# Decoder layer with routed experts on one core: second half's scatter and first half's gather sent one DMA to an expert block, ranks made at tile 11, first block turned behind the last values

## The reference

```python
x = _layernorm(x + attn(x, Wq, Wk, Wv))
x = _layernorm(x + xattn(x, ctx, ctx, mask, Wq, bq, Wk, bk, Wv, bv, Wo, bo))
logits = x @ Wg + bg
topk_vals, topk_idx = jax.lax.top_k(logits, 2)
topk_w = softmax(topk_vals)
h = relu(einsum('bsd,edf->bsef', x, W1) + b1)      # 8 experts, f = 512
eo = einsum('bsef,efd->bsed', h, W2) + b2
y = sum(take(eo, topk_idx) * topk_w) + x
return gamma * (y - mean(y)) * rsqrt(var(y) + 1e-5) + beta
```

## Time and profile before

| what | value |
|---|---|
| median of 3 runs | 957.79 us (957.04 to 963.1) |
| the profiled execution | 955.7 us, span 953.9 us |
| PE busy | 765.7 us, 80% of the span |
| DVE busy | 628.2 us, 66% |
| ACT busy | 457.6 us, 48% |
| POOL busy | 303.2 us, 32% |
| chain that ended last, by engine | PE 59%, DVE 19%, issue 6%, POOL 6%, DMA 5%, ACT 2% |
| indirect DMAs, scatter | 32, mean 982 ns on POOL |
| indirect DMAs, gather | 32, mean 952 ns on POOL |

### The profile page before, as it was taken

How to read it: one execution, slowest core, us unless ns; L and a number is a source line. 1 busy time by engine, 2 the same in 40 slices (tenths; PEclk the granted TensorE clock), 3 DMA queues, 4 the chain that set the end, 5 groups by cost and what they waited for, 6 DMA issues and landing times.

```text
span 953.9 us, 14840 instructions
## 1 busy us (share of the span) xinstructions
PE 765.7 (80%) x4736; PEld 375.7 (39%) x4736; DVE 628.2 (66%) x983; ACT 457.6 (48%) x919; POOL 303.2 (32%) x311
## 2 busy tenths in 40 slices
PE   6767999889999999999888859853994997699700
PEld 3433222222222222222235536532682775477500
DVE  3568788778888888888548977874361432296346
ACT  2211677667777777777665243422341442245300
POOL 6000086967000000000135562737005003264074
PEclk9978899999999999999999979985996999799955
DMA  7661629796504040400007000002222223212231
GB/s 224 164 179 52 146 95 280 251 263 251 89 1 89 1 80 11 77 13 2 0 1 329 23 1 1 0 12 85 76 74 105 69 67 93 87 57 68 85 88 44
DMA packets 53682, 86.64 MB, mean 91 GB/s; under 512 B 16425, under 2 KB 41257, under 8 KB 52457
## 3 DMA queue, kind: packets, MB, share of 16 engines
q1 hardware_dynamic: 41689, 53.25, 20.3%
q0 software_dynamic: 9280, 31.20, 9.9%
q10 hardware_dynamic: 2640, 1.24, 0.6%
HBM read 48.15 MB, written 33.03 MB: 85 GB/s over the span
## 4 chain that ended last, share of the span: by engine, by line
PE 59%; DVE 19%; issue 6%; POOL 6%; DMA 5%; ACT 2%; SPq 2%; POOLq 0%; DVEq 0%; ACTq 0%
PE bank L475 10%; PE bank L483 10%; PE quad L784 10%; PE quad L458 9%; PE bank L798 7%; DVE rowmax L856 6%; PE bank L589 3%; POOL yg L1585 2%; PE quad L560 2%; POOL x_sorted L1535 2%; DVE max L962 2%; DVE sc L957 1%; DVE xres L931 1%; ACT probs L1279 1%; DMA qstack<-negrows 1%
## 5 line engine op out<-in xcount | busy, mean ns | idle before, releaser
L856 DVE TENSOR_REDUCE rowmax<-quad 128x1 f32<-128x1024 f32 x256 | 303.4, 1219 | 73.0 <-PE quad L458 71.6
L1279 ACT ACTIVATE probs<-bank 128x512 f32<-128x512 f32 x512 | 281.7, 595 | 101.3 <-PE bank L475 99.2
L475 PE MATMUL bank<-qstack,kstack 98*128 98x512 bf16 x512 | 194.1, 387 | 15.2 <-ACT probs L1279 9.7
L458 PE MATMUL quad<-kstack,qstack 96*128 96x512 bf16 x512 | 177.3, 386 | 9.2 <-DVE rowmax L856 7.8
L483 PE MATMUL bank<-probs,vslot 128*32 128x512 f32 x1024 | 138.1, 608 | 0.0
L784 PE MATMUL quad<-xbT,w_all 128*128 128x128 bf16 x1104 | 102.6, 226 | 33.4 <-issue 30.5
L475 PEld LDWEIGHTS bank<-qstack,kstack 98*128 98x128 bf16 x512 | 49.0, 97 | 199.4 <-ACT probs L1279 168.9
L784 PEld LDWEIGHTS quad<-xbT,w_all 128*128 x1104 | 76.5, 97 | 60.2 <-issue 45.6
L1388 ACT ACTIVATE xbT<-bank 128x512 bf16<-128x512 bf16 x46 | 27.5, 597 | 138.0 <-PE bank L765 98.5
L1521 POOL TENSOR_TENSOR lnv<-lnv,power 128x4 f32<-128x4 f32 (+1 forms) x8 | 9.6, 1198 | 264.3 <-DVE lnv L909 264.3
L458 PEld LDWEIGHTS quad<-kstack,qstack 96*128 96x128 bf16 x512 | 48.4, 99 | 70.8 <-DVE rowmax L856 34.2
(11 more groups left out here) (169 smaller groups left out, 976.3 us busy)
## 6 DMA issues: line engine op xcount, KB each, us to landing
w_all<-w_split SPq DMA_DIRECT2D x2, 4096.0 KB, 17.5
kstack<-k_parts SPq DMA_DIRECT2D x48, 128.0 KB, 7.2
xb<-x_sorted SPq DMA_DIRECT2D x46, 128.0 KB, 2.2
y_sorted<-ysb SPq DMA_DIRECT2D x46, 128.0 KB, 1.7
x_sorted<-zeros POOLq DMA_DIRECT2D x6, 768.0 KB, 9.0
vslot<-v_all SPq DMA_DIRECT2D x8, 512.0 KB, 8.8
w1raw<-in_w POOLq DMA_DIRECT2D x8, 512.0 KB, 5.2
w2raw<-in_w POOLq DMA_DIRECT2D x8, 512.0 KB, 7.1
```

The costliest lines, as they stand in the source:

```text
L458: mm = pe.matmul(bank[2 * (p % 2) + e], q, kstack[slot][0:MAXROW, j, e * 512:e * 512 + 512], start=True, stop=True)
L475: mm = pe.matmul(bank[4 + i % 2], kstack[slot][0:KROWS, j, kt * P:kt * P + P], qstack[slot][0:KROWS, half, j, :], start=True, stop=True)
L856: dve.tensor_reduce(rowmax[:, k % 2, p:p + 1], quad[:, 2 * (p % 2):2 * (p % 2) + 2, :].rearrange("p a n -> p (a n)"), AX_X, ALU.max).then_ ...
L1279: act.activation(probs[:, i % PR, :], bank[4 + i % 2], ACT.Exp, scale=INV4).then_inc(probs_ready, 1)
```

## The change

- The second half's 16 scatter DMAs each wait for a count of finished blocks, y_done, of 5, 5, 6, 7, ... 18 (SPREAD1). The first half's 16 gather DMAs wait for y_done 24 to 39 (SPREAD0), and those of tiles 6 and 7 stand behind moments(0, 0).
- SP loads blocks 23 and 24 in iteration 18 (17 and 18 before), block 25 in 19, and so on as before.
- Mixing moves: mix of groups 0 and 1 from iterations 29 and 31 to 33 and 41, first_norm from 33 and 35 to 37 and 44, finish_tiles from 37 and 38 to 41 and 45. ORDER has (1, 0) ahead of (0, 1). Group 1's output is stored after the last block.
- rank(0) and rank(1) are made at the end of tile 11 instead of inside tile 12; place(0) moves from the end of VectorE's tile 12 to its start, and copies the ranks out of PSUM first (ranks_taken); the second pair of score matmuls of tile 15 waits for that copy.
- The first scatter is split 8 and 8 DMAs over tiles 12 and 13 instead of 4 and 12.
- values2 of the last group goes ahead of the first block's transposes, and ScalarE's copies likewise. The last group's turns, logits, ranks, low_x2, top_two, place(1) and weigh(1) go one block earlier.

```diff
...
         spot = sb("spot", [P, HT, NE])
+        ranked = sb("ranked", [P, HT + 1, NE])
         spots = sb("spots", [P, 2, HT, NE])
...
         filled, scattered = [sem(f"filled{h}") for h in range(2)], [sem(f"scattered{h}") for h in range(2)]
-        chosen_done, ranks_ready, row_done, tab_done = map(sem, ("chosen_done", "ranks_ready", "row_done", "tab_done"))
+        chosen_done, ranks_ready, ranks_taken, row_done, tab_done = map(sem, ("chosen_done", "ranks_ready", "ranks_taken", "row_done", "tab_done"))
         xb_loaded = [sem(f"xb_loaded{i}") for i in range(XB)]
...
 
-        ORDER = [(0, 0), (0, 1), (1, 0), (1, 1), (0, 2), (0, 3), (1, 2), (1, 3)]
+        ORDER = [(0, 0), (1, 0), (0, 1), (1, 1), (0, 2), (0, 3), (1, 2), (1, 3)]
         MOMENTS = [o for o in ORDER if o[1] < TG - 1]
...
         BLOCKS = 2 * HB
-        MIX, FIRST, LAST, SHOWN = (HB + 6, HB + 8), (HB + 10, HB + 12), (HB + 14, HB + 15), (HB + 17, HB + 18)
+        MIX, FIRST, LAST, SHOWN = (HB + 10, HB + 18), (HB + 14, HB + 21), (HB + 18, HB + 22), (HB + 20, None)
+        SPREAD1, SPREAD0 = [5 + 7 * j // 8 for j in range(2 * HT)], [HB + 1 + j for j in range(2 * HT)]
         QK_JOBS, V_JOBS = 4 * TG, 2 * TG
...
             sp.dma_start(b2[:, :, :].rearrange("p e d -> p (e d)"), t["b2"].rearrange("(o e) d -> o (e d)", o=1).to_broadcast([P, NE * D])).then_inc(b2_loaded, 16)
+            start = {b: max(b - LEAD, HB - 5 + (b - HB) // 2 if b >= HB else 0) for b in range(LEAD, BLOCKS)}
             for m in range(BLOCKS):
-                if m + LEAD < BLOCKS:
-                    load_block(m + LEAD)
+                for b in range(LEAD, BLOCKS):
+                    if start[b] == m:
+                        load_block(b)
                 store_block(m)
-                for g in range(2):
-                    if m == SHOWN[g]:
-                        store_tiles(g, m)
+                if m == SHOWN[0]:
+                    store_tiles(0, m)
+            store_tiles(1, 0)
             store_tiles(2, 0)
...
                         pe.wait_ge(logits_taken, 2)
-                        rank(0)
-                        rank(1)
+                if n == NT - 1 and half == 1:
+                    pe.wait_ge(ranks_taken, 1)
                 for e in (2 * half, 2 * half + 1):
...
                     project_o2(g)
+                if n == NT - 5:
+                    pe.wait_ge(s2_taken, NT - 1)
+                    rank(0)
+                    rank(1)
 
...
 
-            turn_block(0)
             values2(TG - 1)
+            turn_block(0)
             turn_block(1)
...
                 output(m, experts.pop(0))
-                if m in (1, 2):
-                    turn_last(m - 1)
-                elif m == 3:
+                if m in (0, 1):
+                    turn_last(m)
+                elif m == 2:
                     logits2(TG - 1)
-                elif m == 5:
+                elif m == 4:
                     rank(2)
...
                 count, ends, starts = (blocks[:, i, :] for i in range(3))
-                total = RANKS[h][:, HT, :]
+                total = ranked[:, HT, :]
                 dve.wait_ge(ranks_ready, 2 * h + 2)
+                dve.tensor_copy(ranked[:, :, :], RANKS[h]).then_inc(ranks_taken, 1)
+                dve.wait_ge(ranks_taken, h + 1)
                 link(dve.tensor_tensor(fill[:, :, :], total.rearrange("p (e o) -> p e o", o=1).to_broadcast([P, NE, 8]),
...
                 link(dve.scalar_tensor_tensor(spot[:, :, :], starts.rearrange("p (o e) -> p o e", o=1).to_broadcast([P, HT, NE]), float(P),
-                                              RANKS[h][:, 0:HT, :], ALU.mult, ALU.add))
+                                              ranked[:, 0:HT, :], ALU.mult, ALU.add))
                 for j in range(2):
...
                 g, i = n // 4, n % 4
+                if n == NT - 4:
+                    place(0)
                 for m in DIVIDED[i]:
...
                     start_moments(4 * j, 4 * j + 4)
-                if n == NT - 4:
-                    place(0)
                 if i == 3 and g:
...
                     weigh(0)
-                elif m == 3:
+                elif m == 2:
                     low_x2(TG - 1)
-                elif m == 4:
+                elif m == 3:
                     top_two(TG - 1)
-                elif m == 6:
+                elif m == 5:
                     place(1)
-                elif m == 8:
+                elif m == 7:
                     weigh(1)
...
 
-            keep_block(0)
             keep_o2(TG - 1)
+            keep_block(0)
             keep_block(1)
...
                     keep_block(m + 3)
-                if m in (2, 3):
-                    keep_last(m - 2)
-                elif m == 7:
+                if m in (1, 2):
+                    keep_last(m - 1)
+                elif m == 6:
                     exp_gap(1)
...
 
-            def scatter(tiles):
+            def scatter(tiles, after=None):
 
...
                     for j in range(2):
+                        if after:
+                            pool.wait_ge(y_done, after[2 * (n - HT) + j])
                         pool.indirect_dma_start(xs[h], bass.IndirectOffsetOnAxis(ap=rowof[:, j, n:n + 1], axis=0), xrow[:, n, :], None).then_inc(scattered[h], 16)
...
                 if n == NT - 4:
-                    scatter(range(0, 2))
+                    scatter(range(0, 4))
                 elif n == NT - 3:
-                    scatter(range(2, HT))
-            def gather(h):
+                    scatter(range(4, HT))
+            def gather(h, tiles):
 
...
                     pool.wait_ge(ys_stored[i], 16 * len(range(i, (h + 1) * HB, YB)))
-                for i in range(HT):
+                for i in tiles:
                     n = HT * h + i
...
                     for j in range(2):
+                        if h == 0:
+                            pool.wait_ge(y_done, SPREAD0[2 * i + j])
                         pool.indirect_dma_start(yg[:, i, j, :], None, ys[h], bass.IndirectOffsetOnAxis(ap=rowof[:, j, n:n + 1], axis=0)).then_inc(yg_loaded[i], 16)
...
             root(6, NT - 4, NT)
-            scatter(range(HT, NT))
-            gather(0)
+            scatter(range(HT, NT), SPREAD1)
+            gather(0, range(0, 6))
 
...
             for k, g in MOMENTS:
+                if (k, g) == (1, 0):
+                    gather(0, range(6, HT))
                 if (k, g) == (0, 2):
-                    gather(1)
+                    gather(1, range(HT))
                 if (k, g) == (1, TG - 2):
```

6 lines of the change are left out of this document (3 added, 3 removed).

## The result

The changed kernel takes 934.38 us (930.53 to 937.42, 4 runs) against 957.73 (957.04 to 963.1, 4 runs); the ratio is 0.9724, with a 95% interval of 0.9667 to 0.978. Its profiled execution is 933.11 us, its span 931.2. Some executions are in a slower state, which the ratios leave out and the longer medians don't. On others the kernel before has no stall, and the same two kernels take the same time.

A forecast was written before the change was run, and what follows sets the result against it. TensorE was taken to lead the expert stage, stalled twice by bursts of 16 indirect DMAs. Terms -28.1 (spreading), -2 (way in) and +8 (tail) sum to -22.1 us: 933.6 profiled, 935.7 us forecast for the median, range 925 to 951.

The forecast's parts named there:

- The burst's cost: Second half's scatter and first half's gather, 16 indirect DMAs each, hold up TensorE: 15.3 and 16.0 us lost, together 31.3.
- the main term, -28.1: Expert stage: spreading the 32 DMAs over blocks wins back 31.3 us and gives back 3.2.
- rival A: The forecast: a backlog of indirect DMAs hurts, lone ones cost 0 to 0.25 us each; 925 to 943 us, chance 0.65.
- The lone DMA: One indirect DMA for each expert block costs TensorE 0.1 us, 3.2 us for 32.
- B: Expert blocks: each lone DMA still holds TensorE about 0.4 us, 12.8 in all; 945.3 us (943 to 952), chance 0.20.
- C: Cost belongs to each DMA wherever it stands, so 31.3 us only move; 963.8 us, up to 970, chance 0.10.
- B's evidence: During the first scatter, DVE read TensorE's logits only at 660.87, though done at 657.1: signals are delayed too.
- D: Spread DMAs starve behind DVE's casts, last scatter misses its 2 us margin at block 23; about +4, 940 us, chance 0.05.
- The way in: Entry to the expert stage: early ranks, values2 ahead of the first block, hidden(0) at 676.3; -2 us (-5 to +3).
- The tail: Last expert blocks: later mix(1) and first_norm(1) delay the last bias add, gather(1) starts at 26.1; +8 us (+2 to +11).
- no stretch of ten us under 8 us of TensorE between the first block and the last: Sign that the forecast is right: TensorE busy at least 8 of every 10 us throughout the expert blocks.
- The sum: Whole kernel: -28.1 - 2 + 8 = -22.1 us, giving 933.6 for the profiled execution and 935.7 for the median.

The follow-up runs named there:

- Pacing: The kernel before with a 128x256 GpSimd memset ahead of each of 32 scatter and gather DMAs, leaving 1.57 us apart: 930.44 us, ratio 0.97.
- pairs: The changed kernel with the first half's gather sent two DMAs to a block, mixing near its old places, old ORDER: 927.55 us, ratio 0.9974.
- Both: The changed kernel with ranks, place(0), first scatter as before, gather two DMAs to a block, mixing early: ratios 0.9614 and 0.9642 against the kernel before.
- The kernel with small DMAs: Changed kernel's way in, old bursts of 16 and mixing places; scatter DMAs write 128 B of a row, gather DMAs fetch 64 rows: 956.59 us.

## Why the prediction came out, point by point

- **The burst's cost**, 15.3 and 16.0: the same kernel without the stall is quicker by 15.5 (bias adds 0 to 23) and 16.0 (23 to 40: 86.85 and 70.83). Right in size. What the prediction didn't see is that it costs this on some chips only: it took one trace of one chip for the program. That the forecast was met in the first comparison is luck in this respect; on the other kind of chip the main term, -28.1, is nothing. There the prediction's other terms are left, -1.9 + 6.6 from the ruler, +0.5 to the end: 5.1 us on the bad side, where the runs say 1.0018 (0.9975 to 1.0062), which takes in both 5.1 us (1.0054) and nothing.
- **Backlog** (rival A): right in what it said of bursts and lone DMAs. Pacing and pairs remove the stall, and bursts of 4, 8 and 16 cost 0.7, 5 and 16 us. Its reason was not good enough: a DMA takes POOL 0.96 us, and in the burst they already leave 1.27 us apart, so by that number nothing would pile up. What is slower than 1.27 us shows only in the gaps of the stall, 1.4 us apart, and in the 1.57 us that suffice. A's range is also narrower than its own bounds: -5 to +3, +2 to +11 and 0 to 8 us add up to 923.5 to 948.5, not 925 to 943.
- **The lone DMA**, taken at 0.1 us: 163.53 us for the changed kernel on the chip with the stall, 163.31 on the one without, 0.01 us each. The 3.2 us given back were too much. The 2.31 us of the earlier trace rows, its only row, is no effect of a DMA either: on the chip without the stall the same kernel has a hidden layer of 2.31 us at 780.85, with no indirect DMA between 734.4 and 785.7. Rivals B and C fall with this, C by 31 us.
- **B's evidence**, the late logits: a true reading. The 3.8 us were the same stall, on a signal instead of on matmuls. It was evidence for bursts, though, not for lone DMAs.
- **D** didn't come. Of the changed kernel's 16 spread scatter DMAs about half, that at 733.95 among them, touch none of DVE's casts of a hidden block; but the one at 714.61 has a whole cast beside it and took 0.96 us all the same:

```profile
714.61 0.96 POOL L1547 DMA_INDIRECT x_sorted<-attn,rowof  x1 [0.47 <-issue]
```

```profile
714.85 0.43 DVE L1064 CAST hh<-hid 128x512 bf16<-128x512 f32 x1 [1.01 <-ACT hid L1408]
```

No scatter DMA of that trace took over 1.14 us, and on the chip without the stall their median time to landing is 2.4 us, spread as in a burst. By the rule of the Trainium skill's page "SBUF — State Buffer" (the "DVE blocks DMA" trap) a DMA would wait for such a cast if it runs in a two-port mode; which mode it runs in no row shows, and at 0.43 us it could not have cost the 2 or 3 us of D. Block 23 came without a wait: its bias adds stand 4.1 us apart.
- **The way in**, -2: measured -2.4 at hidden(0), -1.74 at the first bias add. The scatter's last DMA started at 669.88, 666.5 without the late start (forecast: ended at 668.4; it ended at 667.5). The forecast named the two parts only as a sum. Apart, values2 ahead of the block is worth -8.4 (54.14 to 45.73) and the early ranks cost +5.9.
- **The tail**, +8: measured +6.86. From bias add 40: mix ended at 5.1, add_beta at 13.2 (14.2 forecast), the last bias add started at 22.2 (22.9), gather(1) at 25.1 (26.1). The mis-sized term is POOL's moments(0,1) with add_beta, 8.0 us from 861.83 and not 9.0. moments(1,1) did not hold gather(1) up: it ended at 880.4, and the last store released gather(1) at 881.65. The sign "no stretch of ten us under 8 us of TensorE between the first block and the last" failed here: TensorE is busy 2.72 us from 870 to 880, and the last block ends at 879.2. That is the tail's own loss, which the prediction had priced but not put into its signs.
- **The sum**: -22.1 forecast, -26.0 on the ruler. The 3.9 us are the lone DMAs (3.2) and the tail (1.1), less the way in. The late start of that execution, a scatter among executions, took 3.3 back; that the profiled execution fell within 0.5 us of the 933.6 forecast for it is owed to that, which is luck.

**Left open.** What the chips differ in, and what holds the signals up. The Trainium skill's page "NOTIFIC — the notification-queue block" (section 3, Interfaces, in its table of ports) says that the block which writes the profiler's records pushes back on those who make them when, in one of its modes, a queue is full, or when one inside it fills, and that this "is what can stall an engine". The stall would then be one of recording. The landing records that are missing in every trace with the stall, and only there, would fit, but lost records and a stall are not one thing: by the same page (section 7.1, Overflow) a queue that is full either loses records or stalls their maker, and the paced kernel lacks the most records while nothing stalls. Against it speaks also that TensorE's records in the stall (three matmuls in 1.4 us) are far fewer than it makes when nothing holds it (about ten matmuls in 1 us). All executions here were recorded, so no run can tell; an unrecorded one of the kernel before on a chip with the stall would. "Both" ran only on chips with the stall; on the other kind 298.6 - 293.8 = 4.8 us less than the kernel before is an estimate from the ruler. The kernel with small DMAs takes 51.2 us to the end and not 49.4; why wasn't looked into.

## What to carry to other kernels

Indirect DMAs from GpSimd in a row can hold up TensorE and the signals to ScalarE and VectorE on some chips; if work runs beside them, leave them 1.6 us apart or send them two to a block of 4 us, and try the distance before moving anything else to make room. Read a stall on a second chip before building on it, and share time out between marks in the program, not between whole spans. Two edits that come as one (early ranks, values2 first) can hide a loss of 5.9 us behind a gain of 8.4.

## What was unexpected of the hardware

- On three or four chips, 16 indirect DMAs 1.27 us apart cost 15 to 16 us of TensorE; 1.57 us apart 0 to 2; on two chips nothing at 1.25 to 1.27. An eighth of the bytes, or half of the rows, changes nothing, and the time on POOL depends little on the rows: 64 take 0.90 us, 128 take 0.95.
- A split on DVE took 2.87 us instead of 0.69 while POOL's add_beta, begun 0.02 us earlier, ran beside it in the changed kernel; four other traces with the same order of mixing have it at the same place (2.72 to 2.87 us):

```profile
837.69 2.87 DVE L1066 TENSOR_TENSOR hl<-hid,hh 128x512 bf16<-128x512 f32 x1
```

```profile
837.67 2.34 POOL L1604 TENSOR_TENSOR xres<-xres,beta_row 128x1024 f32<-128x1024 f32 x1
```
